# Cross-attention and routed FFN on one core: the context loaded with its two last axes exchanged, and split without transpositions

## The reference, cut to what matters

```python
x = x + xattn(ctx, ctx, layernorm(x), mask, wq, bq, wk, bk, wv, bv, wo, bo)
x = x + ffn(layernorm(x), rms_w, gate_w, W1, b1, W2, b2)

def xattn(v, k, q, mask, ...):
    qh, kh, vh = heads(q @ wq + bq), heads(k @ wk + bk), heads(v @ wv + bv)
    logits = einsum('bhqd,bhkd->bhqk', qh, kh) / sqrt(16) + mask * -1e9
    return merge(softmax(logits) @ vh) @ wo + bo

def ffn(x, ...):          # each row goes to the expert of its largest score
    xn = x * rsqrt(mean(x * x) + 1e-6) * rms_w
    scores = softmax(xn @ gate_w.T); e = argmax(scores)
    return (silu(xn @ W1[e] + b1[e]) @ W2[e] + b2[e]) * max(scores)
```

## Time and profile before

| | |
|---|---|
| runs shown, median | 920.2 us (919.24 to 921.61) |
| the profiled execution, its own time | 914.09 us |
| its span from first to last instruction | 912.3 us |
| granted clock of PE, mean | 0.967 |
| PE, DVE, POOL, ACT busy | 802.1, 620.0, 444.6, 430.2 us |
| HBM traffic | 143 GB/s over the span |

### The profile page before, as it was taken

How to read it: one execution, slowest core, us unless ns; L and a number is a source line. 1 busy time by engine, 2 the same in 40 slices (tenths; PEclk the granted TensorE clock), 3 DMA queues, 4 the chain that set the end, 5 groups by cost and what they waited for, 6 DMA issues and landing times.

```text
span 912.3 us, 28391 instructions
## 1 busy us (share of the span) xinstructions
PE 802.1 (88%) x8764; PEld 586.7 (64%) x8764; DVE 620.0 (68%) x1898; ACT 430.2 (47%) x1004; POOL 444.6 (49%) x566
## 2 busy tenths in 40 slices
PE   1678999999999999999999999998627999999994
PEld 0445666666666666666666666665415888888783
DVE  4567777777777777777777877776374666665542
ACT  0235555555555555555555565554403333333331
POOL 0255644565445564456544665465416555556311
PEclk9989999999999999999999999999857999999998
DMA  4465676656776567765777567764153222223200
GB/s 134 108 169 134 171 175 182 177 142 169 180 186 175 142 164 181 204 195 153 196 191 215 165 168 193 195 189 120 32 195 95 77 82 82 81 79 97 71 29 7
DMA packets 107139, 130.01 MB, mean 143 GB/s; under 512 B 12942, under 2 KB 93704, under 8 KB 106569
## 3 DMA queue, kind: packets, MB, share of 16 engines
q1 hardware_dynamic: 100936, 116.38, 47.4%
q0 software_dynamic: 5600, 12.87, 4.7%
q10 hardware_dynamic: 544, 0.00, 0.0%
HBM read 94.07 MB, written 36.06 MB: 143 GB/s over the span
## 4 chain that ended last, share of the span: by engine, by line
PE 33%; SPq 16%; POOL 16%; DMA 15%; issue 10%; DVE 7%; ACT 1%; POOLq 1%; DVEq 0%
DMA arena_w<-in_x 14%; PE ps L1218 12%; PE ps L1236 10%; POOL arena_w L595 6%; SPq L476 5%; SPq L471 5%; POOL arena_b L583 3%; POOL arena_w L602 2%; POOL arena_w L584 2%; POOL arena_b L559 2%; SPq L440 1%; DVE arena_b L1351 1%; PE ps L1018 1%; POOL arena_b L584 1%; PE ps L994 1%
## 5 line engine op out<-in xcount | busy, mean ns | idle before, releaser
L744 ACT ACTIVATE arena_b<-ps 128x448 f32<-128x448 f32 (+1 forms) x384 | 194.0, 540 | 120.0 <-PE ps L980 119.1
L1369 DVE CUSTOM_DVE_ANT_0 arena_w<-ps,arena_w 112x375 bf16<-112x375 f32 x256 | 140.5, 549 | 47.4 <-PE ps L954 41.3
L976 PE MATMUL ps<-arena_b,arena_w 128*128 128x448 bf16 x384 | 136.6, 356 | 7.7 <-DVE arena_b L1378 5.6
L557 POOL TENSOR_TENSOR arena_b<-arena_b,arena_w 112x1 f32<-112x1 f32 x32 | 6.1, 190 | 279.8 <-DVE arena_b L1353 279.8
L1369 DVE CUSTOM_DVE_ANT_0 arena_b<-ps,arena_w 112x375 bf16<-112x375 f32 x256 | 139.8, 546 | 0.1
L980 PE MATMUL ps<-arena_b 128*128 128x224 f16 x768 | 136.2, 259 | 0.0
L1218 PE MATMUL ps<-arena_b,w_parts 128*128 128x256 f16 (+1 forms) x1056 | 109.2, 254 | 0.5 <-issue 0.3
L1218 PEld LDWEIGHTS ps<-arena_b,w_parts 128*128 x1056 | 90.8, 98 | 17.4 <-issue 2.9
L980 PEld LDWEIGHTS ps<-arena_b 128*128 128x128 f16 x768 | 75.2, 98 | 39.4
L994 PE MATMUL ps<-arena_b 128*17 128x112 f32 (+1 forms) x3072 | 99.4, 261 | 0.1
L1236 PE MATMUL ps<-arena_w,arena_b 128*128 x840 | 95.2, 273 | 0.1
(11 more groups left out here) (187 smaller groups left out, 1344.1 us busy)
## 6 DMA issues: line engine op xcount, KB each, us to landing
arena_b<-k_spill SPq DMA_DIRECT2D x128, 192.0 KB, 3.8
arena_b<-in_L_ffn_W SPq DMA_DIRECT2D x64, 256.0 KB, 4.5
arena_b<-q_spill SPq DMA_DIRECT2D x128, 112.0 KB, 4.2
k_spill<-arena_b SPq DMA_DIRECT2D x32, 384.0 KB, 5.0
arena_b<-in_ctx SPq DMA_DIRECT2D x32, 256.0 KB
arena_w<-in_x SPq DMA_DIRECT2D x64, 112.0 KB, 4.6
q_spill<-arena_w SPq DMA_DIRECT2D x32, 224.0 KB, 2.1
rows<-arena_w SPq DMA_DIRECT2D x32, 224.0 KB, 2.3
```

The costliest lines, as they stand in the source:

```text
L744: nc.scalar.activation(probsT[u % PROB_BUFFERS][0:n], scoreT_bank[c][0:n, 0:QUAD * T], ACT.Exp, scale=1.0 / SCALE_SCORES).then_inc(probs_r ...
L976: pe.matmul(bank[:, 0:QUAD * T], mask_keys[:, quad, c, :], max_rows[par].rearrange("p h t -> p (h t)"), start=True, stop=False)
L1369: nc.vector.tensor_tensor_reduce(out=masked_scores[r % 2], in0=shared_bank[r][0:T, 0:S], in1=mask_bias, scale=-1.0, scalar=3.4e38, op0=ALU ...
```

## The change

ctx is handed over as 32 x 256 x 375, so that its rows are features and its columns keys. One DMA per batch loads it into a tile of 128 partitions by 2 by 375, the layout that the transposition used to make. ACT and DVE read that tile in place of PSUM, ACT waits for the load in place of PE, and `transpose_context` is gone. SP waits for `ctx_low_ready` before it reloads the tile. PE's wait for `ctx_low_ready` in quad 0's scores goes, and one for `q_low_ready` stands there; `project_keys` keeps its own wait for `ctx_low_ready`.

```diff
-        ctx_in = [carve("b", P, CHUNKS, D) for _ in range(2)]
+        ctx_in = [carve("b", P, DT, S) for _ in range(2)]
...
-        proj_bank, ctx_bank = shared_bank[0:2], shared_bank[1:3]
+        proj_bank = shared_bank[0:2]
...
-                sp.dma_start(ctx_in[parity][:, 0:CHUNKS - 1], ctx[bass.ds(b, 1), 0:(CHUNKS - 1) * P].rearrange(
-                    "o (c k) d -> k (o c) d", c=CHUNKS - 1)).then_inc(ctx_loaded[parity], 16)
-                sp.dma_start(ctx_in[parity][0:ROWS[-1], CHUNKS - 1], ctx[bass.ds(b, 1), (CHUNKS - 1) * P:S].rearrange(
-                    "o k d -> k (o d)")).then_inc(ctx_loaded[parity], 16)
+                sp.dma_start(ctx_in[parity], ctx[bass.ds(b, 1)].rearrange("o (j p) s -> p (o j) s", p=P)
+                             ).then_inc(ctx_loaded[parity], 16)
...
-                    wait_apart(sp, ctxT_ready, DT * (st.batch(0) + 1), sp_passed)
+                    wait_apart(sp, ctx_low_ready, DT * (st.batch(0) + 1), sp_passed)
...
-            def context_high(b, par, j):
+            def context_high(b, par, half, j):
-                act.wait_ge(ctxT_ready, DT * b + j + 1)
+                act.wait_ge(ctx_loaded[par], 16 * (half + 1))
...
-                nc.scalar.activation(ctx_parts[par][:, 0, j, 0:S], ctx_bank[j][:, 0:S], ACT.Copy
+                nc.scalar.activation(ctx_parts[par][:, 0, j, 0:S], ctx_in[par][:, j], ACT.Copy
...
                     pe.wait_ge(q_parts_ready, 2 * b + 1)
+                    pe.wait_ge(q_low_ready, DT * (b + 1))
                     pe.wait_ge(k_low_ready, DT * (b + 1))
...
-                    if st.exists(-1):
-                        pe.wait_ge(ctx_low_ready, DT * (b + 2))
...
-            def transpose_context(b, par, half, j):
-                pe.wait_ge(ctx_loaded[par], CTX_LOADED * (half + 1))
-                if j == 0:
-                    wait_count(pe, k_low_ready, DT * b)
-                for c in range(CHUNKS):
-                    n = ROWS[c]
-                    mm = pe.transpose(ctx_bank[j][:, c * P:c * P + n], ctx_in[par][0:n, c, j * P:(j + 1) * P],
-                                      ident[0:n, 0:n])
-                mm.then_inc(ctxT_ready, 1)
...
-                if st.exists(-2):
-                    for j in range(DT):
-                        bank_free(st, 3, 1 + j)
-                        transpose_context(st.batch(-2), st.parity(-2), st.half(-2), j)
...
-                nc.vector.tensor_tensor(ctx_parts[par][:, 1, j, 0:S], ctx_bank[j][:, 0:S], ctx_parts[par][:, 0, j, 0:S],
+                nc.vector.tensor_tensor(ctx_parts[par][:, 1, j, 0:S], ctx_in[par][:, j], ctx_parts[par][:, 0, j, 0:S],
                                         ALU.subtract).then_inc(ctx_low_ready, 1)
...
-        a = np.ascontiguousarray(inputs[name])
+        a = np.ascontiguousarray(inputs[name].transpose(0, 2, 1) if name == "ctx_1024" else inputs[name])
```

More of the change, by code:

```diff
@@ L345, in build @@
         res_ready = sem("res_ready")
-        ctxT_ready = sem("ctxT_ready")
         ctx_high_ready = sem("ctx_high_ready")
@@ L433, in build @@
         N_SETUP_COPIED = 6
-        CTX_LOADED = 16 * 2
         @block.sync
@@ L848, in step @@
                     for j in range(DT):
-                        context_high(st.batch(-2), st.parity(-2), j)
+                        context_high(st.batch(-2), st.parity(-2), st.half(-2), j)
                 if st.exists(3):
@@ L853, in _ @@
             for j in range(DT):
-                context_high(0, 0, j)
+                context_high(0, 0, 0, j)
             run_steps(act, step)
@@ L1166, in step @@
                     transpose_maxima(st)
-            for j in range(DT):
-                transpose_context(0, 0, 0, j)
             run_steps(pe, step)
```

## The result

The changed kernel takes 997.2 us (median of 4 runs, 994.3 to 998.4) where the kernel before takes 920.8 (4 runs, 919.2 to 921.6): ratio 1.083, 95% interval 1.081 to 1.085. The forecast was 944 with a range up to 966: the sign and the engine were right, the size was three times too small (+76 us for +24). The profiled execution took 994.3 us, its span is 992.6.

A forecast was written before the change was run, and what follows sets the result against it. It took two rings as the bound: x's load (18.93 us per step), then DVE and PE (18.63). +24.4 in 28 steps, +1.0 and +0.8 at two seams, -1.6 at the start: 938 profiled, 6.1 more for the median, 944; range 909 to 966.

The forecast's parts named there:

- Transpositions worth 0: Six matmuls gone from PE, 0.81 us per step; value 0 on the path, since PE then waits for L1378 anyway.
- x and SP's queue, up to 0.30 us per step: One ctx issue fewer on SP before x, 0.49 us sooner; ends DVE's x wait, gaining at most 0.30 per step.
- ACT, +0.03 us: ACT's L752 reads SBUF in place of PSUM; 0.03 us added for the first of two, bounds 0 and 0.1.
- L1330 held by POOL, as L1385 is: DVE's L1330, now all-SBUF, waits for the POOL instruction under way; bounds 0 and 4 us per step.
- Case C: At the two L1330: no wait for POOL at all; -10 us, median 910, chance 0.15.
- One POOL instruction at each seam (A): Each L1330 waits for one POOL instruction; step 19.8 us, +24.4 over 28 steps, median 944, chance 0.56.
- B: At L1330, one POOL instruction more; 20.9 us per step, +55, median 975; chance 0.17 with mixtures included.
- mixture: The first L1330 waits one POOL instruction more in half the steps; median 960, within the shared chance of 0.17.
- The first L1330 is due 452.09 + 0.15 + 0.03 = 452.27: At the seam, first L1330 waits to 452.51, ahead of L570, whose start is 452.47; a margin of 0.20 us.
- The start, -1.6: Before the loop, DVE's L1330 can run right after DVE's setup, at 24.10 instead of 25.66: -1.6 us.
- L976 at 453.98 + 1.2 = 455.2. The step is 19.8 us: At the seam, PE's L976 starts 1.2 us later behind L1378, making the step 19.8 us against 18.93.
- that idle time as a sign to look for: PE's idle before L976 was to grow from 0.43 to over 1.5 us, with L1378 as its releaser.

The follow-up runs named there:

- e6: e2's kernel with six transpositions that nothing reads put back on PE at their old place; ratio 0.987 to the kernel before.
- e1: Kernel before, with only the first input of DVE's low part (L1330) taken from the loaded context tile in SBUF instead of PSUM; ratio 1.056.
- e4: Kernel before plus a DVE reduction of 1875 elements per step ahead of the spread maxima; ratio 1.110.
- e2: Changed kernel with POOL's split of W1 made to wait for the step's spread maxima; ratio 0.990 to the kernel before.
- e7: e2's kernel with POOL's split of W2 also moved, between the spread maxima and rstd; ratio 0.986 to the kernel before.
- e5: Kernel before, with e2's edit alone: POOL's split of W1 waits for the spread maxima; ratio 0.999.
- e11: Changed kernel with one small POOL instruction (about 0.27 us) ahead of W1's split; ratio 1.103 to the kernel before.
- e3: Changed kernel with seven matmuls, results overwritten, on PE between quad 0's scores and the wait for the spread maxima; ratio 1.045 to the kernel before.
- e10: Kernel before plus a DVE reduction of 2 x 375 elements per step between the low parts and the spread maxima; ratio 1.032.
- e8: The changed kernel again, unaltered, on another chip; ratio 1.084 to the kernel before.
- e14: Changed kernel, w_in buffers exchanged between odd and even steps (the two runs numbered just before: ctx_in, ctx_parts); 1023.5 us, the three 1.07 to 1.08.

## Why the prediction missed, point by point

**Transpositions worth 0.** Right where nothing holds the seam (e6). With the hold their absence lengthens PE's idle time, and what that costs wasn't measured.

**x and SP's queue, up to 0.30 us per step.** Right in size: the wait of bn_stats fell from 40.0 to 2.3 us, and the loop lost 4.9 us by it. But in the changed kernel the longer step alone does that, as e1 and e4 show. The change's own part is seen in e2, e6 and e7, where the step is not longer and the wait is still down to 4.7, 11.1 and 3.5 us: with about 2 us at the start it is the percent (the loop of e6's profiled run is 7.4 us shorter than e5's, its first spread maxima 1.9 us earlier).

**ACT, +0.03 us.** Right: 509 ns in the median for 483.

**L1330 held by POOL, as L1385 is.** Right, and shown from both sides: e1 brings it about by the operand alone, e2 takes it away by the neighbour alone. Case C, the only one in which the kernel would have been faster, hung on taking the rows on L1385 for a matter of single inputs. The Trainium skill's rule ("SBUF — State Buffer", "Who interferes with whom") that two SBUF inputs contend with a GpSimd instruction that reads SBUF is what e1 shows, 550 ns to 1432 in the median. The Trainium skill also says there that issue order decides who blocks; no run here bears that out at the resolution of the trace: e11 has equal starts and different winners.

**One POOL instruction at each seam (A), 0.56 against 0.17 for B or a mixture.** Half right. It was the mixture: 1.96 and 2.92 us in turn, the two values that the prediction gave for A and B (1.9 and 3.0). The first of two steps that failed is here: "The first L1330 is due 452.09 + 0.15 + 0.03 = 452.27, in L569: it waits to 452.51. L570 waits behind it". The placing was right to a few hundredths, POOL's second instruction starts 0.20 us behind the first low part in the even steps and 0.29 in the odd ones, but a margin of 0.20 us was read as won in every step. The term measured 41.4 us in the loop where A alone has 28. By itself that gives about the 960 that the mixture was priced at, inside the range.

**The start, -1.6.** The low parts did start right behind DVE's setup, as worked out, but that setup itself ended 0.8 us later in this execution: 24.83, where 24.10 was forecast and 25.66 was the time before, so 0.8 us were gained, not 1.6. The third spread maxima came 6 us later than before (99.2 for 93.1), since the seams before them were held as well and the first two steps lost clock. (The forecast's own sum, 914.1 + 24.4 + 1.8 - 1.6, is 938.7, where it says 938; the 0.7 us decide nothing.)

**What was missing.** The second step that failed, and the one that took the time out of the range: the prediction's "L976 at 453.98 + 1.2 = 455.2. The step is 19.8 us" takes every matmul behind the seam at its old duration, so that PE's longer wait costs only itself. PE waits longer at the seam (before L976 0.43 us in the even and 0.1 to 0.3 in the odd steps before, 2.4 and 1.4 now), and behind two thirds of the seams it ran at 1.2 GHz for the keys and the first transposed scores, on the path: 37.7 us, nearly as much as the hold itself. The prediction named that idle time as a sign to look for and gave it no price. In the steps from 93 to 603 us the profile before had nothing to read it from, with the clock at 1.00 and 7.58 us in each step. But at its start it did, where PE stands idle for 1.8 us twice:

```profile
45.00:68.00 23.00, 16.27 (x153) 10.76 (x152) 15.08 (x51) 8.78 (x19) 11.62 (x15) 0.84 0.65 174
```
```profile
45.96 0.37 PE L954 MATMUL ps<-arena_b,arena_w 32*112 32x375 f16 x4 [0.73 <-issue]
...
51.25 0.57 PE L954 MATMUL ps<-arena_b,arena_w 32*112 32x375 f16 x4 [1.83 <-DVE arena_w L1344]
```

The window's clock is 0.84, and the same four matmuls take 0.57 in place of 0.37 behind the second wait. A rival in which PE runs at the lower clock behind a longer wait could have been priced from such rows. With this term the spans add up: 912.3 + 41.4 + 37.7 - 4.9 + 6.1 ahead of the third L1356 = 992.6.

In "TensorE: Matmul & The Clock Gate", section "HAM oscillation — how this bites in real kernels", the Trainium skill tells of a kernel in which waits between bursts of matmuls bring the clock down each time. e3, e4 and e10 show the like in this loop, at 1.6 to 2.7 us a seam in the changed kernel, but not each time: 18 of 27 seams lost clock. It would have been the rival to price.

## What to carry to other kernels

A delay that ends in idle time on PE has two prices, its length and what the matmuls behind it take at the lower clock; here the second was 0.36 of the first in e1, 0.73 in e10, 0.81 in e4 and 0.91 in the changed kernel, so a change that lengthens PE's wait once per step should be forecast with both. Before an operand moves from PSUM to SBUF, look at what POOL runs beside that instruction: moving POOL's work into its idle time, one wait, turned 8% slower into 1% faster. And when it hangs on 0.2 us at a seam which of two instructions goes first, price both outcomes as a mixture.

## What the runs showed of the hardware that was not expected

- Whether the clock falls at a seam is not set by the idle time alone: with 0.87 us of it nothing was lost at 403 us and 1.7 us at 442 (e10), with 2.44 us nothing at 360 and 2.6 us at 400 (the changed kernel). Where it fell, a seam lost 1.1 to 2.9 us.
- Seven matmuls of no use, 1.5 us, kept the clock at full speed at all 27 seams (e3); by ratios of two chips the kernel was 3.5% faster for them.
- A DVE instruction that waits for POOL shows the wait as duration (1.65 us for 0.55), not as idle time, and so does a POOL instruction (1.35 for 1.04). The wait tables name neither; the spread of an instruction's durations does.
- Which of the two goes first alternated with the step inside the loop through e1, e3, e8 and e11 to e14 (but for step 3 of e11), whatever the step's length, a small shift of POOL, or the buffers. At the end of step 29, where POOL has left the loop, POOL went first in all of them.
